# Order of the score matmuls in an attention step: both scores of a step directly behind each other

## What is computed

```python
q, k, v = heads(x @ Wq + bq), heads(x @ Wk + bk), heads(x @ Wv + bv)      # 16 heads of 16
scores = einsum('bhqd,bhkd->bhqk', q, k) * scale
sparsity = scores.max(-1) - scores.mean(-1)                               # one number per query
_, top_idx = top_k(sparsity, int(0.6 * 512))
attn = softmax(scores of the chosen queries)                              # the others' output is 0
out = zeros.at[top_idx].set(attn @ v)
x = x + out @ Wo + bo
```

## Time and profile before

| what | us |
|---|---|
| median of three executions | 1763.51 |
| fastest and slowest of them | 1759.76 and 3657.65 |
| the profiled execution | 1756.66 |
| span of the core in it | 1754.9 |

### The profile page before, as it was taken

One profiled execution on the slowest core, in us unless ns is written; L12 is line 12 of the kernel. 1 busy time (PEld: TensorE's weight loads), 2 busy tenths in 40 slices (PEclk: granted clock), 3 DMA queues, 4 the chain that ended last, 5 costly groups with the idle time before them and its releaser, 6 DMA issues.

```text
span 1754.9 us, 25565 instructions
## 1 busy us (share of the span) xinstructions
PE 1517.9 (86%) x8756; PEld 1076.1 (61%) x8756; DVE 1113.9 (63%) x2182; ACT 636.5 (36%) x900; POOL 549.4 (31%) x697
## 2 busy tenths in 40 slices
PE   3788888889887389999999898898989989898987
PEld 2333333333432178888777687786867778677766
DVE  3877787787877855555574664747557474574832
ACT  1266666666666222222322132331223222232211
POOL 5353544444531023421222322122322223322230
PEclk9688999999999689999999899998989989899997
DMA  5122222222221211101100000000000000000000
GB/s 146 46 57 53 66 55 58 60 55 59 48 56 33 88 36 42 43 25 49 31 1 25 1 24 0 14 10 0 24 0 24 0 0 24 0 24 0 0 13 12
DMA packets 52465, 57.15 MB, mean 33 GB/s; under 512 B 15413, under 2 KB 37701, under 8 KB 52413
## 3 DMA queue, kind: packets, MB, share of 16 engines
q1 hardware_dynamic: 38717, 40.18, 8.6%
q0 software_dynamic: 13408, 16.29, 4.1%
q10 hardware_dynamic: 288, 0.00, 0.0%
HBM read 21.81 MB, written 8.90 MB: 17 GB/s over the span
## 4 chain that ended last, share of the span: by engine, by line
PE 50%; issue 21%; DVE 14%; POOL 7%; ACT 5%; DMA 1%; POOLq 0%; DVEq 0%; SPq 0%; ACTq 0%
PE ps L1687 10%; PE ps L1715 9%; PE ps L809 5%; POOL h L1312 4%; PE ps L782 3%; PE ps L796 3%; PE ps L743 3%; DVE mc L496 3%; PE ps L1698 3%; PE ps L1787 3%; PE ps L1727 2%; PE ps L751 2%; PE ps L1673 2%; PE ps L1748 2%; ACT pT0a L670 2%
## 5 line engine op out<-in xcount | busy, mean ns | idle before, releaser
L496 DVE TENSOR_REDUCE mc<-ps 128x2 f32<-128x1024 f32 x256 | 306.3, 1220 | 44.2 <-PE ps L782 44.1
L1715 PE MATMUL ps<-w_hi,h 128*128 128x256 f32 x1024 | 220.1, 298 | 0.9 <-DVE h L1543 0.8
L249 POOL DMA_DIRECT2D k_st<-k_hi x256 | 123.3, 487 | 266.5 <-PE ps L796 251.1
L1687 PE MATMUL ps<-xT_b,w_hi 128*128 128x512 f32 x512 | 180.0, 433 | 0.0
L1603 ACT ACTIVATE h<-ps 128x512 fp32r<-128x512 f32 x128 | 76.4, 597 | 282.3 <-PE ps L1748 282.3
L782 PE MATMUL ps<-k_st,q_st 48*128 48x512 f32 x512 | 137.8, 535 | 37.3 <-DVE mc L496 37.3
L1715 PEld LDWEIGHTS ps<-w_hi,h 128*128 128x128 f32 x1024 | 166.6, 189 | 4.5 <-DVE h L1543 4.3
L1312 POOL TENSOR_TENSOR h<-hf,h 128x512 fp32r<-128x512 f32 x64 | 82.6, 1291 | 253.4 <-DVE h L1554 253.4
L782 PEld LDWEIGHTS ps<-k_st,q_st 48*128 48x128 f32 x512 | 51.9, 199 | 169.3 <-issue 85.9
L1543 DVE SCALAR_TENSOR_TENSOR h<-ps,h 128x512 fp32r<-128x512 f32 x128 | 88.3, 690 | 104.2 <-ACT h L1603 101.4
L1715 PE MATMUL ps<-w_lo,h 128*128 128x256 f32 x512 | 143.2, 280 | 0.0
(11 more groups left out here) (260 smaller groups left out, 3472.3 us busy)
## 6 DMA issues: line engine op xcount, KB each, us to landing
q_st<-q_hi SPq DMA_DIRECT2D x256, 32.0 KB, 2.0
k_st<-k_hi POOLq DMA_DIRECT2D x256, 32.0 KB, 1.9
q_st<-q_lo SPq DMA_DIRECT2D x128, 32.0 KB, 2.1
k_st<-k_lo POOLq DMA_DIRECT2D x128, 32.0 KB, 2.0
x<-in_x_dram SPq DMA_DIRECT2D x8, 512.0 KB, 3.9
x_dram<-x SPq DMA_DIRECT2D x8, 512.0 KB, 2.9
x<-x_dram SPq DMA_DIRECT2D x16, 256.0 KB, 3.8
out_dram<-tok SPq DMA_DIRECT2D x16, 256.0 KB, 3.3
```

Of the source, the lines that this page charges most:

```text
L249: eng.dma_start((q_st, k_st)[which][par][64 * e + DH * r:64 * e + DH * r + DH, j, :].bitcast(F32), src[(2 * j + e) * DH:(2 * j + e + 1) * ...
L496: v.tensor_reduce(mc[par][:, qt, 2 * HU + j:MC:NPAIR], ps[:, at:at + 2, :], AX_X, ALU.max).then_inc(max_done, 1)
L1687: last = t_.matmul(ps[:, bank, :], ws[a][:, c, m * P:(m + 1) * P], xT[s][k][:, c, :], start=n == 0, stop=close and n == NC * len(PASSES) - 1)
L1715: last = t_.matmul(ps[:, ACC[s] + t // 2, (t % 2) * D:(t % 2 + 1) * D], h[s][m % 2][a][:, t * P:(t + 1) * P], ws[k][:, m, :], start=m == 0 ...
```

## The change

In PE's `step`, the second score is issued directly behind the first, ahead of the first half of the transposed scores and of the "E" tasks. The number of instructions, their operands and their waits stay as they are, and no other engine's stream is touched. It acts in the steps that issue two scores: 14 units of 8 steps and 5 steps of unit 14, 117 in all. Steps with one score or none keep their order.

```diff
@@ -895,10 +895,10 @@
 
         def step(u, b, g, p):
             next_scores(u, b, g, 2 * p)
+            next_scores(u, b, g, 2 * p + 1)
             next_scores_T(u, g, p, 0)
             for t in tasks_at(u, g, p, "E"):
                 task(u, b, g, t)
-            next_scores(u, b, g, 2 * p + 1)
             next_scores_T(u, g, p, 1)
             products(u, g, p)
             for t in tasks_at(u, g, p, "L"):
```

## The result

| | before | after |
|---|---|---|
| median, us | 1769.88 (4 executions) | 1842.86 (4 executions, 1839.3 to 1849.25) |
| span of the profiled core, us | 1754.9 | 1837.7 |
| mean granted clock of it | 0.935 | 0.917 |

The changed kernel is slower: ratio 1.0451, 95% interval 1.0398 to 1.0505. Of the four executions before, one of 3657.65 us was disturbed and does not enter the ratio, which is taken against the other three (median 1763.51 us). The spans differ by 82.8 us.

The account below looks back on a forecast made before the run. PE looked like the bound (busy 86%), but PE and DVE wait for each other, and the change closes a loop between them. 1756.66 + 70 + 15 = 1841.7 us, plus 3 for the runs: 1845 us, range 1815 to 1875 us.

Parts of the forecast that it names:

- The two terms: Added to the profiled 1756.66 us: +70 us for longer steps in the units, +15 us for the clock.
- The loop: Second score, transposed scores, task, consumer, DVE's second reduction, next second score: Q 5.03 us against 3.91, K 6.50 us.
- The short steps: Steps with a short task or none: 3.68 us instead of 3.34 for O0, O1, mean and no task; mx 4.27.
- the lost cover: In short steps the second score no longer stands within ACT's exponential and costs its own 0.34 us.
- Unit 14: The last unit adds 0.36 us for V and 4 times 0.34 us: 1.7 us.
- The clock: More stretches at the lower clock behind PE stalls, 82 us in place of 46: +15 us, bounds nothing and 37.
- The other place: Q and X1 steps: one stretch of 3.4 us at the lower clock behind ten of the 21.
- the rival that took it for half of the stage: Clock oscillates through the attention stage, 265 us at the lower level in place of 46: +66 us, 1896 us; chance 0.08.
- That only K's stall would show: Rival: other steps absorb DVE's lateness; K and the step behind cost 2.0 us in 14 units: 28 us, 1788 us; chance 0.06.
- The faster case: Rival: DVE runs both reductions back to back, PE's 37.3 us idle for the maxima goes: 1726 us; chance 0.03.
- its own deciding point: Whether DVE's second reduction starts before the task's consumer; in DVE's stream it stands behind it.
- The signs that were to show it: Profile after: K step 6.5 us, Q 5.0, X1 5.3, short 3.7; PE idle ahead of L782 about 90; DVE busy 1114.

Follow-up runs that it names:

- e3: The changed kernel with one more DVE subtraction, result unused, ahead of the low part of q in each Q step: 1860.25 us, ratio 1.0587.
- e4: The kernel before with one more DVE subtraction, result unused, ahead of the low part of q in each Q step: 1762.57 us, ratio 1.0008.
- e1: The changed kernel with DVE's second reduction directly behind its first, ahead of the task's consumer: 1799.19 us, ratio 1.0223.
- e6: The changed kernel with the second score behind the first transposed half and DVE's second reduction directly behind its first: 1755.09 us, ratio 0.9952.
- e2: The changed kernel with two more zero-weight matmuls in each K step ahead of the products: 1813.01 us, ratio 1.0317.
- e7: The changed kernel with DVE's sum of k and mean weights moved behind the second reduction in K steps: 1834.32 us, ratio 1.041.

## Why the prediction held, point by point

**The total.** 1845 us were forecast, 1842.86 measured, 82.8 us of span against +85 (70 for the steps, 15 for the clock). The two terms were off by 10 and 8 us in opposite directions, so the agreement within 3 us is partly luck.

**The loop.** From first transposed half to first transposed half, medians over seven units at the stated kinds: V 4.63 us (4.65 forecast), Q 5.02 (5.03), K 6.50 (6.50), X1 5.42 (5.33), V with X0 4.89 (4.88). This is the step that the forecast rested on, and it held to 0.1 us, by sums of distances read in a trace in which the loop did not exist yet. e3 and e4 show that the consumer lies in it, and e1 that DVE's order opens it.

**The short steps** were over-forecast: 3.50 to 3.58 us and 4.03 for mx, not 3.68 and 4.27. Two scores directly behind each other take 271.39 - 270.82 = 0.57 us, not 2 times 0.34, and in most of them the two halves stand 1.5 us apart, not 1.59; the four transposes of mx take 0.53 us, not X1's 0.59. What this place costs in all is a different matter: the forecast charged the lost cover with 0.34 us in each of nine short steps a pair, 21 us in all, while one place later takes 3% off the kernel's time (the table under e6), some 50 us, with the clock that follows from it and a loop that is one place shorter. The lengths of the steps held; how the cost divides between the loop and the lost cover they did not say rightly. A pair at full clock is read from e2, whose units 10 and 11 had no low clock: first scores at

```profile
435.67 0.72 PE L784 MATMUL ps<-k_st,q_st 48*128 48x512 f32 x4
...
506.33 0.73 PE L784 MATMUL ps<-k_st,q_st 48*128 48x512 f32 x4
```

so 70.7 us against the 72.2 forecast and 62.5 before: 57 us in seven pairs where 68 were forecast.

**Unit 14** took 2.8 us more, not 1.7.

**The clock** was under-forecast: what is left for it is 82.8 - 57 - 2.8 = 23 us, not 15, though within its bound of 37. The mean from 80 to 580 us fell from 0.96 to 0.89, so from about 40 us (2 x 0.04 x 500) to about 110 us (2 x 0.11 x 500) at the lower level. So some 70 us more at the lower level cost 23 us, a third of a microsecond each, where the forecast had 36 us more and half a microsecond for most of them: the length was too short by half and the price too high. The working had the place behind K right and the length wrong: one stretch of 3.4 us was read from the earlier trace rows, but in nine of the 14 units it was 10.2 us. The other place was wrong: ten of the 21 Q and X1 steps were to have a stretch as well, and in the 14 units none of them has one. The page of the Trainium skill that the prediction names ("TensorE: Matmul & The Clock Gate", section "A second HAM failure mode: psum-queue depth-cycling") describes a clock that swings between its levels as PE idles in short pieces; the trace agrees for the steps behind K (0.50 from 288.4 to 298.5) and not for the rest of the unit, so the rival that took it for half of the stage, 1896 us, did not come.

**The rivals.** That only K's stall would show fell with Q at 5.02 and X1 at 5.42 us. The faster case fell as its own deciding point said: the second reduction starts behind the consumer (279.43 and 285.93). e1 made the two reductions stand together, which gave 1.0223, and e6 shows what that case is worth one place later: half a percent, where 2% were imagined.

**The signs that were to show it.** PE's idle ahead of L782 was to grow to about 90 us and came to 61.0. By steps the trace gives the reason: of the 37.3 us before, 30 stood in the steps behind K and 7 ahead of the first step; the 30 disappeared, as the prediction itself says of this stall, but its 90 adds the new waits to them as if they stayed. The new waits are 54 us where about 65 were counted, since a row holds only what exceeds the 0.3 us in which PE is at its neighbour anyway, 2.34 us in K and 0.85 in Q. The step behind K has no stall ahead of its second score, as forecast. PE's idle ahead of the transposed scores was to grow by 0.3 us in each short step, some 19 us; it grew by 32 us, from the row of the page before

```profile
L796 PE MATMUL ps<-q_st,k_st 64*128 64x512 f32 x512 | 113.2, 438 | 26.7 <-ACT pT0a L670 16.1
```

to 58.6 us. DVE's busy time stayed.

**What is open.** Why the low clock lasts 10.2 us behind K in nine units and 3.4 or 6.8 in the others was not tried; nor was a filler in the Q and X1 stalls, which could tell what they add to it. In units of odd number DVE's work behind K ends last in e1 by the trace; no run takes it away. How the 3% of the score's place divide into cover and clock is open too.

## What to carry to other kernels

When an instruction is issued earlier, look at what its wait hangs on, in the other engine's program order: if the partner does work between the two things it exchanges with you, the late place was that work's slack, and both streams have to be reordered together. Look also at what the instruction now stands ahead of: here the same score one place later, behind the matmul that feeds ACT, was worth 3%. The length of the loop that closes can be added up from a trace in which it is still open. And a stall on PE has to be priced with the clock behind it, while a wait that disappears may uncover a second chain of the same length, here the transfers of stacked k.

## What the runs showed of the hardware beyond that

- More work on PE made the kernel faster: two matmuls with a zero weight of 17 columns in each of 14 stalls took 30 us off the span of 1837.7 (e2), and kept the granted clock from 80 to 580 us at 0.98 in place of 0.89.
- The low clock outlasted its cause: behind a stretch with PE busy 0.47 of 2.80 us it stayed at 0.50 for 10.1 us in which PE was busy 9.26 us.
- From the start of a 1.22 us reduction on DVE to the matmul that waited for its end are 1.26 to 1.28 us in the rows shown, and from POOL's first transfer of stacked k to the matmul that waited for the sixth of them 4.4 us (e7), 4.7 us (e6) and 4.8 us (e1, unit 4 of each).
